# First norm's beta added with its scale on the turned tokens by ScalarE in PSUM instead of by bias products, with three pieces of work put elsewhere

## The reference, cut to what matters

```python
def _L1_gnn_ref(node_features, adjacency_matrix, attn_w, attn_b, W1, b1, W2, b2, g1, beta1, g2, beta2):
    ...
    for l in range(attn_w.shape[0]):
        si = x @ attn_w[l, :d]
        sj = x @ attn_w[l, d:]
        scores = si[:, :, None] + sj[:, None, :] + attn_b[l]
        scores = jnp.where(scores >= 0, scores, 0.2 * scores)
        scores = jnp.where(mask, scores, -jnp.inf)
        attn = jax.nn.softmax(scores, axis=-1)
        agg = jnp.einsum('bij,bjd->bid', attn, x)
        h = layernorm(x + agg, g1[l], beta1[l])
        ff = jax.nn.gelu(h @ W1[l] + b1[l], approximate=False) @ W2[l] + b2[l]
        x = layernorm(h + ff, g2[l], beta2[l])
    return x
```

## Time and profile before

| | |
|---|---|
| median of 3 runs (lowest, highest) | 1562.35 us (1561.89, 1564.15) |
| the profiled execution's own time | 1562.23 us |
| its span | 1560.4 us |
| busy: PE, PEld, DVE, ACT, POOL | 1502.3, 1268.8, 1370.5, 1100.7, 901.0 us |

### The profile page before, as it was taken

One profiled execution on the slowest core, in us unless ns is written; L12 is line 12 of the kernel. 1 busy time (PEld: TensorE's weight loads), 2 busy tenths in 40 slices (PEclk: granted clock), 3 DMA queues, 4 the chain that ended last, 5 costly groups with the idle time before them and its releaser, 6 DMA issues. The chain is left out here.

```text
span 1560.4 us, 35206 instructions
## 1 busy us (share of the span) xinstructions
PE 1502.3 (96%) x11360; PEld 1268.8 (81%) x11360; DVE 1370.5 (88%) x4305; ACT 1100.7 (71%) x1948; POOL 901.0 (58%) x1008
## 2 busy tenths in 40 slices
PE   5899999899999999999999999999999999999995
PEld 3677776788888888888888888888888888888884
DVE  6999999798988899988889999989899999898952
ACT  5788888366767676767676767776767676767663
POOL 5799998335455465645454657363637573645465
PEclk9999999599999999999999999999999999999998
DMA  6533443500000121200011212000112120000001
GB/s 195 165 132 123 133 134 118 176 8 14 8 14 25 31 69 41 62 15 11 12 31 26 75 35 68 8 14 8 32 28 72 37 67 8 14 8 14 8 28 54
DMA packets 70874, 82.79 MB, mean 53 GB/s; under 512 B 29264, under 2 KB 54096, under 8 KB 70736
## 3 DMA queue, kind: packets, MB, share of 16 engines
q1 hardware_dynamic: 69104, 74.76, 16.6%
q0 software_dynamic: 816, 3.15, 0.6%
q10 hardware_dynamic: 816, 3.15, 0.5%
HBM read 38.95 MB, written 25.17 MB: 41 GB/s over the span
## 5 line engine op out<-in xcount | busy, mean ns | idle before, releaser
L849 ACT ACTIVATE bank<-bank,b_col 128x512 f32<-128x512 f32 x384 | 252.9, 659 | 337.2 <-PE bank L763 337.0
L775 PE MATMUL bank<-w_hi,hid_hi 128*128 128x256 f32 x1536 | 442.6, 288 | 12.8 <-DVE hid_lo L1018 12.5
L775 PE MATMUL bank<-w_lo,hid_hi 128*128 128x256 f32 x1536 | 433.9, 283 | 0.0
L775 PE MATMUL bank<-w_hi,hid_lo 128*128 128x256 f32 x1536 | 433.7, 282 | 0.0
L1018 DVE TENSOR_TENSOR hid_lo<-bank,hid_hi 128x512 fp32r<-128x512 f32 x384 | 259.0, 685 | 101.8 <-ACT hid_hi L854 97.1
L775 PEld LDWEIGHTS bank<-w_hi,hid_hi 128*128 128x128 f32 x1536 | 292.2, 190 | 46.7 <-DVE hid_lo L1018 36.3
L763 PE MATMUL bank<-nT_hi,w_hi 128*128 128x512 f32 x768 | 317.0, 413 | 1.2 <-DVE nT_lo L1147 1.2
L763 PE MATMUL bank<-nT_lo,w_hi 128*128 128x512 f32 x768 | 303.2, 395 | 0.0
L763 PE MATMUL bank<-nT_hi,w_lo 128*128 128x512 f32 x768 | 301.7, 393 | 0.0
L775 PEld LDWEIGHTS bank<-w_lo,hid_hi 128*128 128x128 f32 x1536 | 292.8, 191 | 9.6
L775 PEld LDWEIGHTS bank<-w_hi,hid_lo 128*128 128x128 f32 x1536 | 292.8, 191 | 0.0
(11 more groups left out here) (127 smaller groups left out, 3100.8 us busy)
## 6 DMA issues: line engine op xcount, KB each, us to landing
raw_weights<-xin SPq DMA_DIRECT2D x96, 128.0 KB, 2.3
xin<-in_x_dram SPq DMA_DIRECT2D x16, 512.0 KB, 4.0
first_block_out<-x_res SPq DMA_DIRECT2D x16, 512.0 KB, 2.7
second_block_in<-x_act SPq DMA_DIRECT2D x16, 512.0 KB, 3.8
xin<-second_block_in SPq DMA_DIRECT2D x16, 512.0 KB, 3.9
x_fin<-first_block_out SPq DMA_DIRECT2D x16, 512.0 KB, 4.1
out_dram<-x_fin SPq DMA_DIRECT2D x16, 512.0 KB, 2.9
xh_other<-xh SPq DMA_DIRECT2D x128, 33.0 KB, 2.3
```

The source lines that it names most:

```text
L775: mm = pe.matmul(FF[t // 2][:, (t % 2) * D:(t % 2 + 1) * D], a[:, r, t * P:(t + 1) * P], w[:, l, c, :], start=(c == 0 and t % 2 == 0 and p ...
L849: act.activation(h[:], h[:], ACT.Gelu, bias=b1_col[:, l, c:c + 1]).then_inc(s_gelu, 1)
```

## The change

Four things are changed.

- `split_n` on ScalarE is now two instructions for each half: an Identity with scale g1 and bias beta1, PSUM to PSUM in place, and after a wait for it a copy that rounds into `nT_hi`. VectorE's `nT_lo` is a plain subtraction.
- The 96 bias products, their two additions on VectorE, and the two small steps that split beta1 are gone; `b1_col` is loaded as it is.
- At the seam, the scores of slot 1 on VectorE and its exp on ScalarE stand before the first gelu, with `spread(1, 1)` ahead of `turn_n(0, 0)` on TensorE and the turning and aggregation of slot 1 one chunk earlier.
- ScalarE issues the loads of W1 in step 3 instead of step 2.

```diff
 def first_scalar(act, tail):
     def step(tau, t):
-        if isinstance(tau, int) and tau == 2:
+        if isinstance(tau, int) and tau == 3:
             act.wait_ge(q_ld, 64)
             for l in range(L):
                 act.dma_start(raw[:, l].rearrange("p (c f) -> p c f", c=KD),
...
-                def bias(l, cs):
...
-                        for k in range(KD):
-                            for w in (w1_hi, w1_lo):
-                                mm = pe.matmul(bank[0][:, at:at + 2], w[:, l, k, c * P:(c + 1) * P], beta1_parts[:, l, k, :],
...
                 def tail(tau):
-                    if tau == NT + 5:
-                        bias(0, range(CF))
                     if tau == NT + 6:
                         pe.wait_ge(s_samer, 1)
                         pe.wait_ge(q_ev, NT)
                         spread(0, 0)
-                        bias(1, range(CF // 2))
-                    if tau == NT + 7:
-                        bias(1, range(CF // 2, CF))
                     if tau == NT + 8:
                         turn_attn(0, 0)
                     if tau == NT + 9:
                         pe.wait_ge(q_vh, 2 * NT)
                         aggregate(0, 0)
-                        bias(2, range(CF))
                 def before():
+                    spread(1, 1)
                     turn_n(0, 0)
-                    spread(1, 1)
...
-                            if nxt and c == (1 if U == 0 else 0):
+                            if nxt and c == 0:
                                 turn_attn(U + 1, s + 1)
-                            if nxt and c == (2 if U == 0 else 1):
+                            if nxt and c == 1:
                                 aggregate(U + 1, s + 1)
...
                 def split_n(V, s):
                     for k in range(KD):
                         act.wait_ge(s_nT, KD * V + k + 1)
-                        act.activation(nT_hi[:, s % 2, k, :], NT_B[k][:], ACT.Copy, scale=g1_col[:, l, k:k + 1]).then_inc(s_nhi, 1)
+                        act.activation(NT_B[k][:], NT_B[k][:], ACT.Identity, bias=beta1_col[:, l, k:k + 1],
+                                       scale=g1_col[:, l, k:k + 1]).then_inc(s_nfull, 1)
+                        act.wait_ge(s_nfull, KD * V + k + 1)
+                        act.copy(nT_hi[:, s % 2, k, :], NT_B[k][:]).then_inc(s_nhi, 1)
...
                     split_n(0, 0)
-                    act.wait_ge(s_b1, 2)
+                    exp(1, 1)
...
-                            if U == 0 and c == 0:
-                                exp(1, 1)
...
                 def split_n(V, s):
-                        dve.scalar_tensor_tensor(nT_lo[:, s % 2, k, :], NT_B[k][:], g1_col[:, l, k:k + 1],
-                                                 nT_hi[:, s % 2, k, :].bitcast(F32), ALU.mult, ALU.subtract).then_inc(s_nlo, 1)
+                        dve.tensor_tensor(nT_lo[:, s % 2, k, :], NT_B[k][:], nT_hi[:, s % 2, k, :].bitcast(F32),
+                                          ALU.subtract).then_inc(s_nlo, 1)
...
                 def before():
-                    dots_of(0, 2, range(0, 2))
-                    dve.wait_ge(s_bias, L)
...
+                    scores(0, 1)
                     first_part_over(dve)
                     split_n(0, 0)
-                    scores(0, 1)
+                    dots_of(0, 2, range(0, 2))
```

More of the change, by code:

```diff
@@ L107, in graph_net @@
         g1_col = sb("g1_col", [P, L, KD])
-        b1_raw = sb("b1_raw", [P, L, CF])
+        beta1_col = sb("beta1_col", [P, L, KD])
         g1_row = sb("g1_row", [P, L, D])
@@ L153, in graph_net @@
             batt_row = sb("batt_row", [P, H], where=first)
-            beta1_col = sb("beta1_col", [P, L, KD], where=first)
-            beta1_parts = sb("beta1_parts", [P, L, KD, 2], F32R, where=first)
             s_w1 = [sem(f"w1_loaded{l}") for l in range(L)]
@@ L264, in constants @@
                     with nc.allow_non_contiguous_dma(reason="small columns, broadcast rows"):
-                        for at, col, src, n in ((6, beta1_col, beta1, KD), (7, g1_col, g1, KD), (8, b1_raw, b1, CF)):
+                        for at, col, src, n in ((6, beta1_col, beta1, KD), (7, g1_col, g1, KD), (8, b1_col, b1, CF)):
                             if tau == at:
@@ L515, in step @@
                         dve.bn_stats(stats[:, 0, :], xin[:, tau % XR, :]).then_inc(q_s0, 1)
[L516 to L521, removed]
                     scores = tau - 6
@@ L778, in output @@
                     mm.then_inc(s_ff, 1)
-                def bias(l, cs):
[L781 to L787, removed]
-                        for k in range(KD):
-                            for w in (w1_hi, w1_lo):
-                                mm = pe.matmul(bank[0][:, at:at + 2], w[:, l, k, c * P:(c + 1) * P], beta1_parts[:, l, k, :],
-                                               start=(c == 0 and k == 0 and w is w1_hi and l == 0),
-                                               stop=(k == KD - 1 and w is w1_lo), skip_group_check=True)
-                    if cs[-1] == CF - 1:
-                        mm.then_inc(s_bias, 1)
                 def tail(tau):
-                    if tau == NT + 5:
-                        bias(0, range(CF))
                     if tau == NT + 6:
@@ L818, in before @@
                     pe.wait_ge(s_w2lo, NT - HEAD)
-                    for done, count in ((q_hT, NT), (q_xh, NT), (q_asd, 3 * NT), (q_vs, 2 * NT), (q_cp, NT), (s_b1, 2)):
+                    for done, count in ((q_hT, NT), (q_xh, NT), (q_asd, 3 * NT), (q_vs, 2 * NT), (q_cp, NT)):
                         pe.wait_ge(done, count)
@@ L1177, in before @@
                 def before():
-                    dots_of(0, 2, range(0, 2))
-                    dve.wait_ge(s_bias, L)
-                    products = bank[0][:, 0:2 * L * CF].rearrange("p (l c e) -> p l c e", l=L, e=2)
-                    dve.tensor_tensor(b1_col[:], products[:, :, :, 0], b1_raw[:], ALU.add).then_inc(s_b1, 1)
-                    dve.wait_ge(s_b1, 1)
-                    dve.tensor_tensor(b1_col[:], products[:, :, :, 1], b1_col[:], ALU.add).then_inc(s_b1, 1)
+                    scores(0, 1)
                     first_part_over(dve)
                     split_n(0, 0)
-                    scores(0, 1)
+                    dots_of(0, 2, range(0, 2))
                 def some(i, which, last):
```

2 lines of the change are left out of this document (1 added, 1 removed).

## The result

The changed kernel takes **1565.72 us** (median of 19 runs, 1564.2 to 1567.64) against 1562.35 for the kernel before, timed beside it (19 runs, 1560.78 to 1564.77). The ratio is 1.0019, 95% interval 1.0013 to 1.0026: 3.4 us slower by the medians, where 6.8 more had been forecast. The profiled execution took 1567.64, with a span of 1565.8.

What follows compares the result with a forecast made beforehand. The second part was taken to run at TensorE's pace, held up once a slot waiting for low(7); 1562.23 - 2.0 - 3.5 + 12.3 = 1569.0 us, forecast 1566 to 1572 (55%), stated range 1558.5 to 1573.5.

Steps and rivals of the forecast that it cites:

- The slot: In 44 slots, the later gelu makes the first dot miss the gap between GpSimd's halves: 0.28 each, 12.3 us lost.
- - 2.0 - 3.5: The forecast gains in us: 2.0 in the first tiles and 3.5 at the seam.
- the split's 1.2 at the seam: At the seam, ScalarE's pairs give back 1.2 us, because the remainder waits for both halves.
- The seam, "gain 3.5": At the seam, removing the products and the exp wait gains 3.5 us, bounds 1.5 and 4.5.
- The 1.65 ahead of the first hidden product: At the seam, slot 0's first hidden matmul moves from 303.72 to about 302.1, 1.65 us earlier.
- the wait for the exp: At the seam, TensorE no longer stands 1.88 us at 311.06 for the exp, which needed table loads around it.
- the return of the clock: At the seam, sooner work could bring TensorE's full clock back sooner; named for the upper bound, 4.5 us.
- The first tiles, "I take 2.0, and nothing gives it back": In the first tiles, the first turned tile precedes the attention columns; 2.0 us gained and kept, bounds 0 and 2.8.
- the late dot costs almost nothing: Rival in the slots: Identity takes 0.66, the dot still makes the gap, 2.2 us lost, total 1558.9; 16%.
- the whole delay passes: Rival in the slots: low(7) follows low(6) step by step, 44 x 0.73 = 32 us lost, total 1588.9; 4%.
- The gains don't last: Rival: a later load catches up the first tiles' 2.0, or the seam gives 1.5; total 1573.0 us; 8%.
- part of the loss: Rival: only mask slots get dots in, or gaps are longer; 6 to 8 us lost, total 1562.5 to 1565.5; 17%.

Runs made afterwards that it cites:

- Experiment 4: The changed kernel with ScalarE's copy of the second half of the turned tokens made twice; 1568.09 us, ratio 1.0029.
- experiment 7: The changed kernel with ScalarE's split halves behind the casts of chunks 5 and 6, VectorE's remainders behind low(5) and the first dot; 1553.64 us, ratio 0.9943.
- experiment 5: The changed kernel with W1's loads issued a step earlier, as in the kernel before; 1566.59 us, ratio 1.0020.
- experiment 11: The changed kernel with the bias products on TensorE and parts of beta on VectorE still computed, read by nobody; 1569.58 us, ratio 1.0038.
- experiment 1: The changed kernel again, unchanged, for a second profile; 1566.06 us, ratio 1.0020.
- 6: The changed kernel, without bias products and with the new split, but with the seam's old order; 1567.14 us, ratio 1.0024.
- experiment 10: The kernel before without the bias products and all that served them, beta left out of the hidden layer; 1556.28 us, ratio 0.9958.

## Why the prediction was right, and where not

**The slot was right, to the mechanism and nearly to the hundredth.** The Identity was taken at 0.755 and has a mean of 0.754 (the other estimate given, 0.80, was 0.05 too high); the gelu of chunk 6 was to come 0.73 late and came 0.70 late, counted from the `low(7)` ahead; a slot was to lose 0.28 and loses 0.26, with a mask 0.29. Experiment 4 excludes that the delay itself is passed on; experiment 7 does ScalarE's whole work and loses nothing, so it is the place of the first dot that costs, not the work. Where exactly it decides, two slots with a mask show that differ by hundredths, slot 9 of the changed kernel's first profile and slot 11 of its second, each the second half of L935 and the first dot:

```profile
559.62 1.28 POOL L935 TENSOR_TENSOR raw_weights<-raw_weights,c_row 128x512 f32<-128x512 f32 x1
...
559.64 1.55 DVE L1032 CUSTOM_DVE_ANT_0 raw_weights<-xin,att_row 128x256 f32<-128x256 f32 x1
```

```profile
612.16 1.56 POOL L935 TENSOR_TENSOR raw_weights<-raw_weights,c_row 128x512 f32<-128x512 f32 x1
...
612.15 0.41 DVE L1032 CUSTOM_DVE_ANT_0 raw_weights<-xin,att_row 128x256 f32<-128x256 f32 x1
```

The dot that starts 0.01 ahead of the half gets in at its full speed, and the half takes 0.26 more; the dot that starts 0.01 to 0.02 behind waits for the whole half. The slot in which it got in took 25.88 in place of 26.08. The same comes once more in experiment 5 (slot 11) and once in experiment 11 (slot 23), each with the dot 0.01 ahead, 0.41 for the dot, 1.56 for the half and a slot of 25.88; no dot that started behind the half got in. The prediction had the last good start at 0.01 behind the half. The Trainium skill ("SBUF — State Buffer", section "Who interferes with whom") calls it an exclusive lock, not a shared bandwidth: these rows agree. A mask slot misses by 0.01 to 0.06 us, an ordinary one by 0.15.

**Where the other microseconds are.** The stages in us, worked out from the starts of the norm of tile 15, the first hidden product, and `low(7)` of slots 0 and 44. Before and changed are means over the two profiles of each; experiment 3 is before with the new split, experiment 2 the changed kernel with the old one.

```
                             before    exp. 3    exp. 2   changed   changed-before   forecast
to the norm of tile 15        71.11     71.28     69.89     70.01        -1.10         -2.0
to the first hidden product  232.17    233.77    229.84    230.76        -1.42         -1.65
to low(7) of slot 0           31.18     31.79     28.22     28.12        -3.05         -1.85
44 slots                    1132.93   1143.53   1131.46   1143.86       +10.93        +12.3
to the end of the span        93.27     93.00     93.06     93.02        -0.25          0
sum                         1560.66   1573.36   1552.48   1565.76        +5.1         +6.8
```

**The step that failed is the size of the gains**, the "- 2.0 - 3.5" of the sum, and of them the 3.5 at the seam above all. To compare like with like, the split's 1.2 at the seam, which the 3.5 had taken off, has to be put to the split: forecast were gains of 6.7 (2.0 + 2.85 + 1.88) and a cost of 13.5 (12.3 + 1.2). Measured are gains of 8.0 (experiment 3 against 1) and 8.8 (experiment 2), and a cost of 12.5 (experiment 1 against 2) and 11.6 (experiment 3). So the gains were 1.3 to 2.1 larger and the split 1.0 to 1.9 cheaper. Together that is 3.1 to 3.2, what the 3.6 of that batch (1566.06 - 1562.45) lack to the forecast 6.8. In the profiles experiment 2 gains 8.2 on before: 1.2 in the first tiles (forecast 2.0), 2.3 up to the first hidden product (2.85), 3.0 behind it (1.88), 1.5 in the slots and 0.2 at the end (nothing forecast). The terms:

- *The seam, "gain 3.5".* It was 4.5 by the profiles, the upper bound given. The 1.65 ahead of the first hidden product are nearly right (1.42). What was too small is what follows it, 3.05 in place of 1.85: I had put down the wait for the exp alone, and named the return of the clock as a bound only. In the first profile of before the clock went from 0.50 (1.2 GHz) to 1.00 (2.4 GHz) 6.0 behind the first hidden product, in those of the changed kernel 4.3 and 6.2 behind. In the second profile of before it rose after 5.3, at 308.2, and was down a second time from 311.6 to 315.0 (the granted clock is the third column from the end):

```profile
306.00:308.00 2.00, 2.00 (x6) 1.29 (x4) 0.00 (x1) 1.96 (x3) 1.81 (x2) 0.50 0.87 297
308.00:310.00 2.00, 0.31 (x1) 0.00 (x0) 0.00 (x0) 1.97 (x3) 2.00 (x3) 0.95 0.19 61
310.00:312.00 2.00, 1.81 (x8) 1.56 (x9) 1.17 (x3) 1.97 (x3) 1.15 (x1) 0.90 0.00 0
312.00:314.00 2.00, 2.00 (x11) 1.94 (x10) 1.05 (x3) 1.97 (x5) 0.00 (x0) 0.50 0.00 0
```

  and in the changed kernel not (its first profile):

```profile
304.00:306.00 2.00, 2.00 (x8) 1.41 (x6) 1.21 (x5) 1.30 (x3) 1.07 (x1) 0.69 0.64 169
306.00:308.00 2.00, 2.00 (x21) 1.28 (x21) 0.52 (x2) 1.25 (x2) 2.00 (x3) 1.00 0.17 64
308.00:310.00 2.00, 2.00 (x16) 1.86 (x15) 1.97 (x3) 1.16 (x2) 2.00 (x2) 1.00 0.22 50
```

  Ahead of the second fall TensorE stood still for most of 308 to 310 (0.31 busy), waiting for the exp. The same happened in experiment 3. But in the first profile of before it stood still for the exp as long (1.88), from just before the clock rose, and the clock stayed up:

```profile
308.00:310.00 2.00, 1.18 (x3) 0.36 (x2) 0.00 (x0) 1.95 (x3) 2.00 (x2) 0.56 0.26 94
310.00:312.00 2.00, 0.94 (x5) 0.85 (x6) 0.93 (x3) 1.97 (x3) 2.00 (x3) 1.00 0.03 10
```

  So the standstill alone doesn't bring the second fall. Where it came, this stage took 31.90 and 31.79, where it didn't, 30.46, and in the changed kernel 28.12: of the 3.05 some 0.7 are the second fall, the rest is gained without it. In the eleven profiles of the changed kernel and the kernels made from it or without products there was none. With the products or the old order alone (experiments 11 and 6) it didn't come, so which of the two prevents it isn't shown.

- *The first tiles, "I take 2.0, and nothing gives it back".* The first product did come 1.9 earlier, but the norm of tile 15 only 1.1. And even these are not due to the first product's start: in experiments 5 and 10 that product came at 14.35 and 14.21, about as before, and the norm of tile 15 still at 70.38 and 70.25. With the loads at the old place and VectorE's two steps on beta, it is 70.99 to 71.28 in three profiles; with the loads at the new place and these steps kept (experiment 11) 69.92. So moving the loads or taking the steps away brings most of the gain, each without the other; why is open. W1's loads, issued at 11.34 on ScalarE, hold the second tile's copy there until 12.97; that this is what gave it back is argued, not shown.

```profile
11.34 1.59 ACTq L368 DMA_DIRECT2D raw_weights<-in_L_gnn_W_dram  x3
12.97 0.37 ACT L388 COPY hT<-bank 128x256 f32<-128x256 f32 x1 [2.91 <-issue]
```

- *The slots of the kernel before, not thought of.* There slots 27 and 32 take 0.24 to 0.31 more than their neighbours, in both profiles and in experiment 3. In experiment 10 they don't, and in the changed kernel neither. It isn't the products by themselves: in experiment 11, which has them, slot 27 takes 25.98 and slot 32 26.04, beside 25.97. What makes them long is open. They are 0.55 of what lies between the slots' term of the split, 12.4 (experiment 2 to the changed kernel), and the 10.9 from before to changed; about half of what is left are seven slots of 25.63 or 25.64 in experiment 2 where before has 25.71.

**From 5.1 in the profiles to 3.4 in the runs** no profile leads. Both profiled executions of the changed kernel are the longest of their runs (1567.64 of 19, 1567.54 of 11), while that of before (1562.23) was at its median. My sum was made against one profiled execution. The runs differ, loosely, with the time at the lower clock: of the 19, the three with a mean granted clock of 0.987 took 1565.25 on average, the five with 0.984 and 0.985 took 1566.8; but the fastest of all (1564.20) had 0.986. That fits a stretch at half clock of variable length, seen in the profiles (it ended at 305.2 and 306.8 in the two of the changed kernel, and `low(7)` of slot 0 came 0.8 later after the first hidden product in the second). That the remaining 1.7 are this is argued, not shown.

The rivals: *the late dot costs almost nothing* fell with the Identity at 0.754 and the period of 25.97; *the whole delay passes* fell with experiment 4. *The gains don't last* is half right for the first tiles and wrong at the seam. The result is at the edge of *part of the loss*, but for another reason than its own: a slot loses nearly all that was forecast (0.26 and 0.29 of 0.28), and the gains are larger. That the total still lies in the range is in part luck: the seam's larger gain and the slots' smaller sum pull it down, the first tiles' smaller gain up.

## What to carry to other kernels

Look at where a late operation arrives, not at how much work is added: the same 1.3 us more of ScalarE work a slot cost nothing in halves under two covers, and 12 us over the run in one piece, through one dot that started 0.15 behind a GpSimd operation. Such a loss is a step: a longer delay cost no more (experiment 4), and bringing the dot back ahead of the half gave it all back (experiment 7). And an engine's busy time doesn't tell what its work costs: the 96 products kept TensorE busy for 17.7 to 19.0 us, mostly at half clock, and putting them back cost 2.9 to 3.9. Without them TensorE is busy 13.65 of 30.80 us in that stretch, so most of their time had lain in waits. What to read is which input they delay.

## What the runs showed of the hardware that was not expected

- A VectorE dot and a GpSimd addition, both from SBUF, are decided by who starts first, within 0.01 to 0.02 us (0.41 against 1.55 for the dot, 1.56 against 1.28 for the addition; three dots that got in, in three profiles).
- An Identity with scale and bias by pointer, PSUM to PSUM, 128x512, takes 0.754 us; the gelu with one pointer 0.660, the copy into SBUF 0.588.
- TensorE's clock, once back at its full level, can fall again: after 2.00 us with TensorE busy 0.31 it did, though TensorE was then fully busy (granted 0.90, then 0.50 with 2.00 of 2.00 busy). In another execution of the same kernel, with a standstill of the same 1.88 us, it did not.
- Two slots in 48 took 0.24 to 0.31 longer than their neighbours in every profile of one program, and not in another that differs only hundreds of microseconds ahead of them (experiment 10). Why is open.
